# Experts of a 16-expert feed-forward layer read as exchanged 32x32 blocks and turned on VectorE, in place of a turned copy in DRAM

## The reference

```python
x, itok_B_0_63, itok_B_0_15        # (64, 128, 512), (64,), (64,)
# layer 0
x = x + einsum('bsd,bdh->bsh', x, W[cat_ids]) + b[cat_ids][:, None, :]
# layer 1, HID = 2048, 384 shared columns, 128 expert columns
h = gelu(einsum('bnd,hd->bnh', x, fc1_w) + fc1_b, approximate=False)
shared = einsum('bnh,sh->bns', h, fc2_w) + fc2_b
expert_x = einsum('bnh,bph->bnp', h, experts_w[indices]) + experts_b[indices][:, None, :]
x = x + concatenate([shared, expert_x], axis=-1)
```

## Time and profile before

| | |
|---|---|
| median of the runs | 1757.18 us |
| lowest and highest of 3 runs | 1754.25 and 1759.35 us |
| span of the profiled execution | 1768.6 us |
| mean granted TensorE clock | 0.995 |
| TensorE matmul busy | 97% |
| VectorE, ScalarE, GpSimd busy | 55%, 33%, 12% |
| DMA engines, queue of SP and of ScalarE | 42.2% and 6.2% |
| bytes moved | 246.13 MB, mean 139 GB/s |

### The profile page before, as it was taken

The page is one execution under the profiler, slowest core; times in us unless marked ns, Lnnn a source line. Parts: engine busy times, 40 slices in busy tenths (PEclk is TensorE's granted clock), DMA queues, the critical chain, the costliest instruction groups (busy, mean ns, idle before and its releaser), DMA issues.

```text
span 1768.6 us, 26735 instructions
## 1 busy us (share of the span) xinstructions
PE 1714.2 (97%) x7681; PEld 1383.7 (78%) x7681; DVE 972.8 (55%) x1688; ACT 583.3 (33%) x991; POOL 205.4 (12%) x198
## 2 busy tenths in 40 slices
PE   6999999999999999999999999999999999999999
PEld 5777778788787878878787887878878787887887
DVE  6544534655555565555556565565556546555554
ACT  5444443333232333323233232333333333333321
POOL 1200100200202020020201002020110202002010
PEclk9999999999999999999999999999999999999999
DMA  8888785444535444453444435443443544445121
GB/s 272 264 255 264 237 252 154 134 104 133 134 95 147 114 130 113 121 143 92 142 130 116 110 109 150 114 143 105 139 113 107 143 116 129 107 122 147 54 66 48
DMA packets 296858, 246.13 MB, mean 139 GB/s; under 512 B 145636, under 2 KB 219508, under 8 KB 296820
## 3 DMA queue, kind: packets, MB, share of 16 engines
q1 hardware_dynamic: 277956, 211.31, 42.2%
q10 hardware_dynamic: 18864, 34.35, 6.2%
HBM read 212.02 MB, written 33.55 MB: 139 GB/s over the span
## 4 chain that ended last, share of the span: by engine, by line
PE 75%; DMA 8%; SPq 6%; DVE 5%; issue 3%; ACT 1%; POOL 1%; DVEq 0%; ACTq 0%
PE ps_out L776 33%; PE ps_h L761 18%; PE ps_e L761 14%; PE ps_y L748 7%; DMA resid<-in_L_cond_experts_b 3%; DMA turn_in<-in_L_cond_experts_w 2%; SPq L317 2%; PE ps_t L678 2%; DMA exp_t<-turn_out 2%; PE ps_e L678 2%; SPq L345 1%; DVE resid L620 1%; DVE h L561 1%; SPq L355 1%; DVE w_split L561 1%
## 5 line engine op out<-in xcount | busy, mean ns | idle before, releaser
L776 PE MATMUL ps_out<-w2e,h 128*128 128x512 f32 x3072 | 770.6, 398 | 0.0
L776 PEld LDWEIGHTS ps_out<-w2e,h 128*128 128x128 f32 x3072 | 575.4, 189 | 135.9
L761 PE MATMUL ps_h<-y_t,w 128*128 128x512 f32 x1728 | 426.9, 397 | 1.4 <-DVE y_t L561 1.4
L761 PEld LDWEIGHTS ps_h<-y_t,w 128*128 128x128 f32 x1728 | 323.0, 188 | 75.0 <-DVE y_t L561 1.6
L608 DVE CAST h<-g_raw 128x512 fp32r<-128x512 f32 x256 | 123.9, 484 | 449.2 <-ACT g_raw L508 449.2
L761 PE MATMUL ps_e<-y_t,w 128*128 128x512 f32 x1344 | 331.2, 396 | 0.0
L761 PEld LDWEIGHTS ps_e<-y_t,w 128*128 128x128 f32 x1344 | 253.4, 189 | 60.3
L480 ACT CAST w2e<-e_raw 128x512 fp32r<-128x512 f32 x224 | 139.0, 621 | 375.7 <-PE ps_out L776 375.7
L748 PE MATMUL ps_y<-w_split,x_t 128*128 128x512 f32 x744 | 219.5, 404 | 25.7 <-DVE x_t L561 23.0
L561 DVE TENSOR_TENSOR w_split<-w_raw,w_split 128x512 fp32r<-128x512 f32 x256 | 179.3, 701 | 79.1 <-ACT w_split L462 78.9
L601 DVE CAST w2e<-w2e 128x512 fp32r<-128x512 f32 x256 | 120.3, 470 | 141.2 <-PE ps_out L776 141.2
(11 more groups left out here) (54 smaller groups left out, 574.7 us busy)
## 6 DMA issues: line engine op xcount, KB each, us to landing
w_raw<-in_L_cond_W SPq DMA_DIRECT2D x256, 256.0 KB, 3.3
e_raw<-exp_t SPq DMA_DIRECT2D x448, 128.0 KB, 2.4
b_all<-in_L_cond_b SPq DMA_DIRECT2D x64, 256.0 KB, 3.7
turn_in<-in_L_cond_experts_w ACTq DMA_DIRECT2D x64, 256.0 KB, 4.9
exp_t<-turn_out ACTq DMA_DIRECT2D x64, 256.0 KB, 5.2
out<-resid SPq DMA_DIRECT2D x64, 256.0 KB, 2.1
x_blocks<-in_x SPq DMA_DIRECT2D x240, 64.0 KB, 2.5
x_raw<-in_x SPq DMA_DIRECT2D x60, 256.0 KB, 3.9
```

What stands on the lines that cost most here:

```text
L761: last = nc.tensor.matmul(h_bank(c, direct)[:, :], w1[:, w, k, c * P:(c + 1) * P], y_t[:, a, k, :, :].rearrange("p b s -> p (b s)"), start ...
L776: last = nc.tensor.matmul(ps_out[b][:, :], h[:, c % 2, a, b * S:(b + 1) * S], fc2_columns(c, c % 2, w, b), start=(c == 0 and n == 0), stop ...
```

## The change

The turned copy in DRAM, its 64 turns on TensorE and the turns of the groups' own chunks are removed, and with them DIRECT: all groups run one body, groups 1 to 14 in the loop. Experts are read straight from the input in every group, as x is: for four chunks at a time (a quad), each of the four batches' experts in four transfers of 64 KB, one for each 32 partitions, in rows of 128 bytes, into `e_blocks`. VectorE turns one chunk of all four batches into `e_whole` (`turn_e`, 128x512), one chunk ahead, between `e_low` and `h_high`; `e_high` and `e_low` read `e_whole`.

So that a transfer's source has few enough dimensions the hidden units are taken in another order: the four chunks of a quad lie 512 hidden units apart (`hidden_rows`); fc1's tiles, fc2's tiles and fc1's bias follow that order. A quad's 16 transfers are issued in two halves of eight, in steps 1, 2, 5, 6, 9, 10, 13 and 14; the quad of the next group's first four chunks goes out in steps 13 and 14, and for group 0 ahead of layer 0's last weight. The tiles of fc1 and fc2 that are turned in group 0 use two load slots in place of three and go to `ps_t` in place of `ps_e`.

```diff
-    PAIR = 2
-    NP = NC // PAIR
+    QUAD = 4
...
-    NQE = HID // D
-    NTURN = exp_w.shape[0] * NQE
-    DIRECT = 2
-
-    exp_t = nc.dram_tensor("exp_t", [exp_w.shape[0], P, NC * PART], F32, kind="Internal").ap()
...
-        e_raw = sb("e_raw", [P, 2, GB, PAIR * P])
-        turn_in = sb("turn_in", [P, 2, D])
-        turn_out = sb("turn_out", [P, 2, D])
-        b1_rows = turn_out[0:NC, 0, 0:P]
+        e_blocks = sb("e_blocks", [P, 2, GB, QUAD * P])
+        e_whole = sb("e_whole", [P, GB * P])
...
         def prep_bank(t):
-            return ps_out[t % GB] if t < PREP_FIRST else ps_e
+            return ps_out[t % GB] if t < PREP_FIRST else ps_t
+
+        def prep_slot(t):
+
+            return t % PSLOTS if t < PREP_FIRST else t % 2
+
+        def prep_tile(t):
+
+            return g_raw[:, 1, :] if prep_slot(t) == 2 else prep_raw[:, prep_slot(t), :]
+
+        def prep_earlier(t):
+
+            return [u for u in range(t) if prep_slot(u) == prep_slot(t)]
...
+        def hidden_rows(c):
+
+            return (c % QUAD) * (NC // QUAD) + c // QUAD
+
         def prep_src(t):
             if PREP[t][0] == "fc1":
-                m = PREP[t][1]
+                m = hidden_rows(PREP[t][1])
                 return fc1_w[m * P:(m + 1) * P, :]
             _, n, q = PREP[t]
-            return fc2_w[n * P:(n + 1) * P, q * D:(q + 1) * D]
+            return fc2_w[n * P:(n + 1) * P, :].rearrange("p (k u h) -> u p k h", k=QUAD, h=P)[q]
 
...
-        def experts_arrived(g, pr):
-            return 16 * GB * (g * (NP // 2) + pr // 2 + 1)
-
-        def experts_whole(c, direct):
-
-            if direct:
-                return ps_e[:, :].rearrange("p (q v n) -> p q v n", q=GB // 2, v=2)
-            off = (c % PAIR) * P
-            return e_raw[:, (c // PAIR) % 2, :, off:off + P].rearrange("p (q v) n -> p q v n", v=2)
-
-        def h_bank(c, direct):
-
-            return ps_h if direct or c % 2 else ps_e
+        def experts_arrived(g, quad):
+            return 16 * GB * (P // Q) * (g * (NC // QUAD // 2) + quad // 2 + 1)
+
+        def h_bank(c):
+
...
-            plan, t = {}, 0
-            for g, before, last in ((0, (2, 6, 7, 9, 10), NC), (1, (1, 2, 3, 5, 6, 7), NC - 4)):
-                for c in range(last):
-                    places = ["before"] * (c in before) + ["after"] + ["within"] * (0 < c < NC - 1)
-                    plan[g, c] = {}
-                    for place in places:
-                        plan[g, c][place] = t
-                        t += 1
-            assert t == NTURN
-            return plan
...
-            for g in range(DIRECT):
-                body(g, True, True)
-            with eng.Fori(DIRECT, NG - 1) as g:
-                body(g, True, False)
-            body(NG - 1, False, False)
+            body(0, True)
+            with eng.Fori(1, NG - 1) as g:
+                body(g, True)
+            body(NG - 1, False)
...
         def load_prep(eng, t):
             if t is None:
                 return
-            after(eng, prep_turned, t - PSLOTS + 1)
-            eng.dma_start(prep_raw[:, t % PSLOTS, :], prep_src(t)).then_inc(prep_in[t % PSLOTS], 16)
+            after(eng, prep_turned, max(prep_earlier(t), default=-1) + 1)
+            dst = prep_tile(t) if PREP[t][0] == "fc1" else prep_tile(t).rearrange("p (k h) -> p k h", k=QUAD)
+            eng.dma_start(dst, prep_src(t)).then_inc(prep_in[prep_slot(t)], 16)
...
-            def load_experts(g, pr, idx, direct):
-
-                if direct:
-                    after(sp, e_turned, g * NC + PAIR * (pr - 1))
-                else:
-                    after(sp, e_lo, g * NC + PAIR * (pr - 1))
-                source = exp_w if direct else exp_t
-                for b in range(GB):
-                    sp.dma_start(e_raw[:, pr % 2, b, :], source[bass.ds(idx[b], 1), :, pr * PAIR * P:(pr + 1) * PAIR * P]
-                                 .rearrange("o p n -> (o p) n")).then_inc(e_in[pr % 2], 16)
+            def load_experts(g, quad, idx, batches):
+
+                after(sp, e_turned, g * NC + QUAD * (quad - 1))
+                if first(g) and quad == 1:
+                    sp.wait_ge(b1_turned, 1)
+                for b in batches:
+                    for i in range(P // Q):
+                        src = exp_w[bass.ds(idx[b], 1), :, :]\
+                            .rearrange("o (j q) (c u i r) -> u i q c (o j) r", q=Q, c=QUAD, i=P // Q, r=Q)[quad, i]
+                        sp.dma_start(e_blocks[i * Q:(i + 1) * Q, quad % 2, b, :]
+                                     .rearrange("q (c j r) -> q c j r", c=QUAD, r=Q), src).then_inc(e_in[quad % 2], 16)
 
...
-                    load_experts(0, 0, first_experts, True)
+                    load_experts(0, 0, first_experts, range(GB))
...
-            def body(g, more, direct):
+            def body(g, more):
                 idx = first_experts if first(g) else [index(exps, g * GB + b, exp_w.shape[0]) for b in range(GB)]
 
                 for c in range(NC):
-                    if c % PAIR == 1 and not (first(g) and c == 1):
-                        load_experts(g, c // PAIR, idx, direct)
+                    if c % QUAD in (1, 2):
+                        batches = range(2) if c % QUAD == 1 else range(2, GB)
+                        if c + QUAD < NC:
+                            load_experts(g, c // QUAD + 1, idx, batches)
+                        elif more:
+                            next_idx = {b: index(exps, (g + 1) * GB + b, exp_w.shape[0]) for b in batches}
+                            load_experts(g + 1, 0, next_idx, batches)
                     load_prep(sp, prep_in_step(g, c))
                     if c == WSLOTS and not first(g):
...
-            for g in range(DIRECT):
-                body(g, True, True)
-            for i in range(2):
-                sp.wait_ge(turn_stored[i], 16 * (NTURN // 2))
-            with sp.Fori(DIRECT, NG - 1) as g:
-                body(g, True, False)
-            body(NG - 1, False, False)
+            groups(sp, body)
...
-            def e_high(g, c, direct):
-                if direct:
-                    after(act, e_turned, g * NC + c + 1)
-                elif c % PAIR == 0:
-                    after(act, e_in[(c // PAIR) % 2], experts_arrived(g, c // PAIR))
+            def e_high(g, c):
+                after(act, e_turned, g * NC + c + 1)
                 after(act, fc2_done, (g * NC + c - 1) * GB)
-                nc.scalar.copy(experts_of(c % 2, 0), experts_whole(c, direct)).then_inc(e_hi, 1)
+                nc.scalar.copy(experts_of(c % 2, 0), e_whole[:, :].rearrange("p (q v n) -> p q v n", q=GB // 2, v=2))\
+                    .then_inc(e_hi, 1)
...
-            def load_tile(t):
-                e, q = t // NQE, t % NQE
-                act.dma_start(turn_in[:, t % 2, :], exp_w[e, :, q * D:(q + 1) * D]).then_inc(turn_loaded[t % 2], 16)
-
-            def copy_tile(t):
-
-                if t is None:
-                    return
-                act.wait_ge(tile_turned, t + 1)
-                after(act, turn_stored[t % 2], 16 * (t // 2))
-                nc.scalar.copy(turn_out[:, t % 2, :], ps_t[:, :]).then_inc(tile_copied, 1)
-                if t + 2 < NTURN:
-                    load_tile(t + 2)
-                act.wait_ge(tile_copied, t + 1)
-                e, q = t // NQE, t % NQE
-                act.dma_start(exp_t[e, :, q * D:(q + 1) * D], turn_out[:, t % 2, :]).then_inc(turn_stored[t % 2], 16)
-
...
-            def gelu(g, c, direct):
+            def gelu(g, c):
                 after(act, fc1_done, g * NC + c + 1)
                 after(act, h_lo, g * NC + c - 1)
-                nc.scalar.activation(g_raw[:, c % 2, :], h_bank(c, direct)[:, :], ACT.Gelu, bias=b1[:, c:c + 1])\
+                nc.scalar.activation(g_raw[:, c % 2, :], h_bank(c)[:, :], ACT.Gelu, bias=b1[:, hidden_rows(c):hidden_rows(c) + 1])\
                     .then_inc(gelu_done, 1)
...
+            def turn_e(g, c):
+                if c % QUAD == 0:
+                    quad = c // QUAD
+                    after(dve, e_in[quad % 2], experts_arrived(g, quad))
+                after(dve, e_lo, g * NC + c)
+                off = (c % QUAD) * P
+                nc.vector.transpose(e_whole[:, :], e_blocks[:, (c // QUAD) % 2, :, off:off + P]).then_inc(e_turned, 1)
+
+            def e_low(g, c):
                 after(dve, e_hi, g * NC + c + 1)
-                minus(experts_of(c % 2, 1), experts_whole(c, direct), experts_of(c % 2, 0)).then_inc(e_lo, 1)
+                minus(experts_of(c % 2, 1), e_whole[:, :].rearrange("p (q v n) -> p q v n", q=GB // 2, v=2),
+                      experts_of(c % 2, 0)).then_inc(e_lo, 1)
 
...
+            turn_e(0, 0)
...
-                    e_low(g, c, direct)
+                    e_low(g, c)
+                    if c + 1 < NC:
+                        turn_e(g, c + 1)
+                    elif more:
+                        turn_e(g + 1, 0)
...
-            def turn_e(g, c):
```

(36 more changed lines are left out.)

53 lines of the change are left out of this document (17 added, 36 removed).

## The result

| | before | changed |
|---|---|---|
| median of the runs | 1756.97 us | **1796.37 us** |
| lowest and highest of 4 | 1754.25 to 1759.35 | 1793.81 to 1797.83 |
| ratio, with 95% interval | | 1.021 (1.0195 to 1.0224) |
| span of the profiled execution | 1768.6 us | 1795.3 us |
| mean granted TensorE clock | 0.995 | 0.968 |

The changed kernel is 39.4 us slower, where 11.2 was forecast: the sign was right, the size was not, and 1796.37 lies just above the range's end of 1796.

A forecast was written before the change was run, and what follows sets the result against it. TensorE bounds the kernel, with no slack where it waits on the expert biases. Start +8.7, group 0 -27.9, group 1 -21.6 and groups 2 to 14 +52.0 sum to +11.2 us: median 1768.4 us, range 1730 to 1796.

The forecast's parts named there:

- What bounds the kernel: TensorE, busy 1714.2 of 1768.6 us; a later group's one idle spot, 1.30 us before slice 4, ends the expert-bias chain.
- Added on SP's queue: Eight expert loads at 0.79 us each ahead of the biases, in place of four, cost 4.0 us a group.
- the last part of the prediction: Signs to look for: y's wait for GpSimd over 6 us a group, TensorE's idle time before slice 4 at 5 to 6.
- a microsecond added ahead of the bias loads is a microsecond of TensorE: At the idle spot before slice 4, delay of the biases passes one for one to TensorE in each group.
- The start and groups 0 and 1: First fc1 8.7 us later; group 0 112.9 for 140.8 us (-27.9); group 1 107.8 for 129.4 us (-21.6).
- the difference is applied to the median: The forecast change in span, +11.2 us, was added to the runs' median, 11.4 us below the profiled span.
- VectorE's turns at nothing: 256 turns of 128x512 on VectorE, 11.2 us a group, fit in its wait for the gelu and cost nothing.
- DMA share near 0.55: With 128-byte packets at 12.6 ns each, the DMA engines' share in a group rises from 0.44 to near 0.55.
- Rival 1: The last bias lands in 2.8 us instead of 4.1, so 2.9 us a group and 1753.0 us; chance 0.15.
- Rivals 2 and 3: Expert DMAs cost SP only 0.52 us, 1737.5 us; or the wait does not grow, 1712.4 us; chance 0.08 each.
- Rival 4: Pieces 2 KB apart go slower, 0.95 us an expert DMA, 5.5 us a group, 1792 us; chance 0.14.

The follow-up runs named there:

- e8: The kernel before, unchanged, profiled a second time: 1756.16 us, span 1754.3 us.
- e1: The changed kernel with the expert biases issued ahead of the eight expert loads of their step: 1692.47 us, 0.9609 of the kernel before.
- e2: The kernel before with the expert biases issued ahead of the four expert loads of their step: 1739.1 us, 0.9869 of the kernel before.
- e3: The kernel before with five unused 64 KB DMAs in 128-byte pieces ahead of the biases in groups 1 to 15: 1833.13 us, 1.0418.
- e4: The changed kernel with 48 identity transposes, results unread, on TensorE ahead of slice 4: 1773.81 us, 1.0073 of the kernel before.
- e7: The changed kernel with expert loads issued last in their step and each VectorE expert turn of groups 1 to 15 made twice: 1697.09 us, 0.9627.

## Why the prediction was right in sign and wrong in size

Measured against e8, whose span (1754.3) and time (1756.16) lie at the median of before; all in us:

| term | forecast | measured | |
|---|---|---|---|
| start, to group 0's fc1 | +8.7 | +10.3 | 51.65 for 41.39 |
| group 0 | -27.9 | -24.1 | 116.6 for 140.7 |
| group 1 | -21.6 | -16.8 | 110.95 for 127.73 |
| groups 2 to 14 | +52.0 | +71.5 | 1423.2 - 1351.7 |
| sum | +11.2 | +40.9 | 1795.3 - 1754.3 = 41.0, with 0.1 in group 15 |

- **What bounds the kernel** was read rightly: one spot without slack, at the end of the chain from the biases. e1, e2 and e3 show it from three sides.
- **Added on SP's queue** held. An expert DMA takes SP 582 ns (median of 1024), eight stand 0.77 apart and occupy SP for 5.97 us, and the biases go out 4.1 us later (4.3 forecast, with the stores). The landing did get faster, by more than was put: from the first bias's issue to GpSimd it is 5.45 us on average of groups 2 to 14, against 6.17 in the profile shown and 5.83 in e8. The ground given for it, fewer bytes ahead of the biases, was wrong: eight loads of 64 KB are as many bytes as four of 128 KB, spread over 6 us instead of 2. The idle time ahead of slice 4 grew to 5.2 us in a loop group, from 1.8 in the profile shown and 1.4 in e8: by 3.4 or 3.8, where 4.0 was put. So this term was right, and if anything a little high. Waits of VectorE and TensorE came to 6.0 and 5.3 a group, as named in the last part of the prediction.
- **The step that failed is the one from idle time to group time**: "a microsecond added ahead of the bias loads is a microsecond of TensorE". The sum has no term for the clock: matmuls behind the idle time were taken at full speed, without a reason. Where the clock stays up this holds: the group of before that idles for 2.74 us takes 105.2 us, 3.0 more than the 102.2 of a group in which nothing waits (e1, e2). In the changed kernel's group 11, 5.00 us of idle time cost 109.2 - 102.2 = 7.0 us, 1.4 for each. The idle time takes the granted clock down, and the matmuls behind it pay 1.6 to 1.8 us more in each group (e4). Against e8 a loop group grew by 3.8 us of idle time and 1.7 of clock, 5.5 in all, where 4.0 and nothing were forecast. 13 x 1.5 = 19.5 us is the miss in the loop, of 29.8 in all. The rows to see it in were there: the earlier trace rows shows the 1.30 idle of a group at clock 1.00, but groups of 106 to 107 us stood among those of 103.8, and I took the undisturbed one for all and did not ask what made the others longer.
- **The start and groups 0 and 1.** Against the profile shown, fc1 came 7.2 later, 8.7 forecast, but that profile was itself late: SP reaches the expert loads at 29.24 us in the changed kernel, at 31.74 in the earlier trace rows and at 29.45 in e8. Against e8, slice 15 starts 9.1 us later (46.70 for 37.59), and the half clock adds 1.2: it is 4.95 us from slice 15 to fc1, and 3.80 in the kernel before. Group 0 was 3.7 longer than the 112.9 forecast, with a clock of 0.96: its first fc1 takes 5.46 us, where one at full clock takes 2.96. How much of the 3.7 is clock was not separated. Group 1 was 3.2 longer than the 107.8 forecast, 1.6 of it clock (e4's group 1 is shorter by that). Most of the rest is idle time ahead of slice 4, 6.52 us here: SP still issues expert loads for 3.8 us behind the group's first fc1 (until 172.11) and reaches the biases 21.0 us behind it (189.31), where it is 19.05 in group 11. Why the queue runs late there was not tested.
- **The base.** Seen against the profile shown, the forecast span was 1779.8 and the measured one 1795.3: 15.5 short (start -1.5, group 0 +3.7, group 1 +3.2, groups 2 to 14 61.9 for 52.0 = +9.9, and rounding). The rest of the miss is the step "the difference is applied to the median": it took off 11.4 us that the changed kernel doesn't give back. In the profile of before they were a later start, longer idle times and half clock in four groups, of which e8 has less; in the changed kernel groups 1 to 14 all have them, and its four executions lie 4 us apart at most (1793.81 to 1797.83).
- **VectorE's turns at nothing**: right (e7). **DMA share near 0.55**: 0.53 in the loop.
- **Rival 1** (the landing faster by 1.3 us) happened for a third to a half, 0.4 to 0.7 us, and was outweighed by the clock. **Rivals 2 and 3** (0.52 us an issue, no growth) fell by the rows above. In the chances, four fifths of 0.55 and all of 0.14 are 0.58, where 0.60 stands.
- **Rival 4** named a time, 1792, that is near the measured one, by a mechanism that didn't occur: in the loop SP issues at 0.77 a DMA. Here is a packet's price, in the DMA view of the stretch from 1278.1 to 1284.1 us:

```profile
q1 hardware_dynamic: 3463, 0.92, 70.7%
```

0.707 x 16 x 6.0 / 3463 = 19.6 ns a packet on average, with 255 larger ones of other loads among them. Whether the pieces 2 KB apart cost more than the 12.6 ns of the x blocks can't be told from it, but they stay under the 24.7 at which it would have mattered. The Trainium skill (DMA: Bandwidth & Descriptors, Measured) gives 0.95 us for a transfer of 64 KB, measured on DMAs that GpSimd issued. Here it is not reached: an estimate from the average is 512 x 19.6 / 16 = 0.63 us of the engines for one load. Eight are issued in 6 us and land a median of 2.6 us after their issue.

## What to carry to other kernels

When a kernel's loads all go through one queue, the place of four small transfers in it can decide over a whole rewrite: ask for each added load who stands behind it, and put first what ends a chain without slack; here two moved lines turned 2.1% slower into 3.9% faster. Where TensorE waits in each round, price the wait by its idle time and by what the matmuls behind it do at the clock that is then granted, and look for rounds of the profile in which that has already happened. And compare rounds with each other before taking one for all: here the uneven ones held the missing term.

## What the runs showed of the hardware

- Behind idle times of 4.7 to 5.0 us in a TensorE stream that is otherwise full, the slice took 1.64 to 1.65 us instead of 0.85 and 12 matmuls 4.07 to 4.39 instead of 2.96, in each group; behind 3.17 and 3.28 the slice took the same and the 12 matmuls 3.82 and 3.62; behind 1.30 and 0.34 they ran at full speed (0.96 and 2.96). In between the length alone did not decide: behind 2.17 us the 12 matmuls took 3.96, behind 2.74 they took 2.96.
- 48 transposes through TensorE in that time kept the granted clock at 1.00.
- VectorE turns 128x512 fp32 in 32x32 blocks in 0.71 us, and a second such turn in each step of groups 1 to 15 (e7) cost nothing that could be measured.
- In e1 TensorE is busy for 1328.80 of 1328.80 us over 13 groups at a DMA share of 0.57: neither 64 small DMAs a group nor their 128-byte pieces show on it.
- SP is held 0.58 us by each of these DMAs and starts one every 0.77 us, where it starts a 128x256 load every 0.52 (four in 1.88). Behind eight of them the biases went out 6.2 us after the first of the eight, behind four 128x256 loads 2.1.
